# Attention scores and their sums one place earlier, and the residual of the first chunk added behind a copy

## The reference

```
x = x + attention(layernorm(x), ctx, ctx)    # 32 query heads, 8 key/value heads of width 128,
                                             # logits capped by 30*tanh(l/30), masked, softmax, then Wo
x = x + ffn(layernorm(x))                    # W_base, bias, and a top-2-of-8 mix of rank-16 LoRA experts
```

## Time and profile before

| | us |
|---|---|
| median of 3 runs (2152.28 to 2160.96) | 2158.23 |
| the profiled execution's own time | 2158.16 |
| its span, first to last instruction | 2156.4 |
| PE busy | 2132.3 |
| DVE busy | 1674.3 |
| ACT busy | 883.1 |
| POOL busy | 294.0 |

### The profile page before, as it was taken

One profiled execution on the slowest core, in us unless ns is written; L12 is line 12 of the kernel. 1 busy time (PEld: TensorE's weight loads), 2 busy tenths in 40 slices (PEclk: granted clock), 3 DMA queues, 4 the chain that ended last, 5 costly groups with the idle time before them and its releaser, 6 DMA issues.

```text
span 2156.4 us, 26390 instructions
## 1 busy us (share of the span) xinstructions
PE 2132.3 (99%) x9429; PEld 1729.3 (80%) x9429; DVE 1674.3 (78%) x2571; ACT 883.1 (41%) x1342; POOL 294.0 (14%) x359
## 2 busy tenths in 40 slices
PE   9999999999999999998999999999999999999999
PEld 7888888888888888876777877777787777888887
DVE  6976888888886666676877779997999879857443
ACT  3323243222241111155565556655666556423221
POOL 0350001111131000012101111111112111100000
PEclk9999999999999999999999999999999999999999
DMA  8698697665596665698666885689767965696741
GB/s 327 234 332 290 218 334 271 231 221 211 209 339 229 211 212 201 221 279 263 189 193 196 233 224 174 202 273 276 194 195 221 298 182 163 210 368 265 294 184 66
DMA packets 207987, 508.50 MB, mean 236 GB/s; under 512 B 20720, under 2 KB 54128, under 8 KB 205808
## 3 DMA queue, kind: packets, MB, share of 16 engines
q1 hardware_dynamic: 187376, 443.31, 62.7%
q0 software_dynamic: 20480, 63.50, 9.3%
HBM read 357.26 MB, written 149.16 MB: 235 GB/s over the span
## 4 chain that ended last, share of the span: by engine, by line
PE 87%; DMA 7%; DVE 3%; ACT 1%; issue 1%; SPq 0%; POOL 0%; DVEq 0%; ACTq 0%
PE ps L377 28%; PE ps L378 28%; PE ps L379 28%; DMA RB<-rD 3%; DMA rD<-r 2%; PE ps L920 1%; DMA X2D<-stg 1%; DMA raw<-gran 1%; DVE Y L990 1%; DMA Y<-xT 1%; DVE Rl L330 1%; DVE ps L330 0%; DVE ps L905 0%; DVE Pl L330 0%; DMA kraw<-ctxT 0%
## 5 line engine op out<-in xcount | busy, mean ns | idle before, releaser
L377 PE MATMUL ps<-Ah,Rh 128*128 128x512 f32 x1024 | 400.9, 391 | 4.2 <-DVE Y L990 4.2
L378 PE MATMUL ps<-Al,Rh 128*128 128x512 f32 x1024 | 399.9, 391 | 0.0
L379 PE MATMUL ps<-Ah,Rl 128*128 128x512 f32 x1024 | 399.5, 390 | 0.0
L379 PE MATMUL ps<-Xq,qW 128*128 128x512 f32 x896 | 348.6, 389 | 0.0
L377 PE MATMUL ps<-Xq,qW 128*128 128x512 f32 x896 | 348.5, 389 | 0.0
L378 PE MATMUL ps<-Xq,qW 128*128 128x512 f32 x896 | 348.5, 389 | 0.0
L330 DVE TENSOR_TENSOR Rl<-raw,Rh 128x1024 fp32r<-128x1024 f32 x174 | 212.2, 1220 | 57.6 <-ACT Rh L326 57.2
L326 ACT ACTIVATE Rh<-raw 128x1024 fp32r<-128x1024 f32 x176 | 185.5, 1055 | 154.6 <-PE ps L379 127.1
L377 PEld LDWEIGHTS ps<-Ah,Rh 128*128 128x128 f32 x1024 | 193.2, 189 | 46.8 <-DVE Y L990 4.6
L379 PEld LDWEIGHTS ps<-Ah,Rl 128*128 128x128 f32 x1024 | 193.1, 189 | 40.8
L378 PEld LDWEIGHTS ps<-Al,Rh 128*128 128x128 f32 x1024 | 193.2, 189 | 40.5
(11 more groups left out here) (217 smaller groups left out, 3881.7 us busy)
## 6 DMA issues: line engine op xcount, KB each, us to landing
raw<-gran SPq DMA_DIRECT2D x177, 512.0 KB, 5.6
QSD<-qW SPq DMA_DIRECT2D x64, 512.0 KB, 3.1
qD<-qt SPq DMA_DIRECT2D x128, 256.0 KB, 3.3
qW<-QSD SPq DMA_DIRECT2D x64, 512.0 KB, 3.7
qf<-qD SPq DMA_DIRECT2D x64, 512.0 KB, 8.5
RB<-rD POOLq DMA_DIRECT2D x128, 256.0 KB, 6.8
qraw<-gran SPq DMA_DIRECT2D x48, 512.0 KB, 4.3
kD<-kst SPq DMA_DIRECT2D x32, 512.0 KB, 3.8
```

What stands on the lines that cost most here:

```text
L377: put("pe", waits, lambda e: e.matmul(pe_out, lh, rh, start=first, stop=False, skip_group_check=more))
L378: put("pe", [], lambda e: e.matmul(pe_out, lh, rl, start=False, stop=False, skip_group_check=more))
L379: return put("pe", [], lambda e: e.matmul(pe_out, ll, rh, start=False, stop=last, skip_group_check=more), mark)
```

## The change

```diff
@@ o_evac @@
                 y = Y[:, n, :]
+                if (c, g) == (0, 0):
+                    a = put("act", [m] + y_free[n // 2], lambda e: e.activation(y, ps[b][:, :], ACT.Copy), cn("act_o"))
+                    bank_free[b] = [a]
+                    y_acc[c, n] = [tt("flex", y, y, Y2[:, n, :], ALU.add, [a, y_marks[c, n // 2]], "y")]
+                    y2_free.append(y_acc[c, n][0])
+                    return
                 a = put("dve", [m, y_marks[c, n // 2]] + y_acc.get((c, n), []),
                         lambda e: e.tensor_tensor(y, ps[b][:, :], y, ALU.add), cn("dve_y"))
@@ plan @@
         first = {0: ((-15, -14, -13, -12), -11, -9, (-7, -6, -5, -4)),
-                 1: ((-11, -9, -7, -6), -4, -2, (2, 3, 5, 6)),
+                 1: ((-11, -9, -7, -6), -4, -2, (1, 2, 4, 5)),
                  2: ((-4, -3, -1, 2), 4, 6, (8, 10, 12, 14))}
         for gi in range(len(groups)):
-            z = 8 * gi - 21
-            scores, sums, rows, values = first.get(gi, (range(z, z + 8, 2), z + 8, z + 11, range(z + 13, z + 21, 2)))
+            z = 8 * gi - 22
+            scores, sums, rows, values = first.get(gi, (range(z, z + 8, 2), z + 8, z + 12, range(z + 14, z + 22, 2)))
@@ at t == -2 @@
                     for j in range(4):
-                        y_load(0, j)
+                        y_marks[0, j] = dma(Y2[:, 2 * j:2 * j + 2, :], xT[0][:, 2 * j:2 * j + 2, :], y2_free, f"d_y{j}", 512)
```

## The result

| | before | changed |
|---|---|---|
| median, 15 runs each (us) | 2153.73 | 2169.97 |
| lowest to highest | 2146.58 to 2164.20 | 2161.86 to 2178.99 |
| the profiled execution, its span | 2158.16, 2156.4 | 2165.07, 2163.3 |

The changed kernel is slower: ratio 1.0069, 95% interval 1.0052 to 1.0085. The time lies above the range given, and the sign is the other one. The profiled execution of the changed kernel is at the fast end of its runs (2165 in 2162 to 2179), and that of the kernel before is above its median, so the two spans differ by 6.9 us where the medians differ by 16.2. The traces show the kinds of loss, but only part of the typical amount.

What follows compares the result with a forecast made beforehand. PE, busy 2132.3 of 2156.4 us, was taken as the bound, leaving only its waits and halved-clock stretches to win. 2158.2 - 4.5 (part one) - 0.9 (three waits) = 2152.8, predicted 2153 us; range 2144 to 2163.

Steps and rivals of the forecast that it cites:

- In all other groups PE never waited for an exponential, a bank or Al: Attention groups away from the three waits: bunching scores and sums takes some cover, cost 0, up to 3 us.
- the three changes of chunk: Near 1270, 1505 and 1737 us, where PE's sums waited for an exponential, 6.5 us together before the change.
- The chain moved with its start: Chain from a group's sums to RB: starting 2.7 us earlier, it was to end DVE's hold 2.7 us earlier.
- the second rival: RB lands no sooner while sums ask 2.7 us earlier; three waits grow 2.7 us each: 2163.5 us, chance 0.17.
- the draining picture: Small DMAs in RB's chain land only when loads in flight have drained, whenever issued; basis of the 2163 us rival.
- The waits at the changes of chunk: Three waits for exponentials were to be about 2.5, 0.5 and 2.8 us, 0.9 us won, slow clock left.
- The shorter hold of DVE: First change of chunk: DVE's hold for RB was to be some 5.4 us in place of 8.12.
- Part one: First chunk's x through Y2: removes place 3's 4.2 us wait and 1.7 us clock loss; 4.5 us won net.
- the 1.4 us wait at place 4: Group 2's sums were to wait 1.4 us for a late exponential, with the clock staying full.
- the three known waits: The sums' waits for exponentials near 1270, 1505 and 1737 us: 0.3 us won at each, 0.9 us together.
- the term put at 0: Cover lost by bunching work at even places in other groups: cost 0, up to 3 us.

Runs made afterwards that it cites:

- the first trace: Profile of the changed kernel itself, against the kernel before: profiled execution 2165.07 us, span 2163.3; median of its runs 2169.97 us.
- The run with stores counted late: Changed kernel with its planner counting each store X2D<-stg as landing 5 us later: 2146.30 us, ratio to the kernel before 0.9963.
- Sums back at -13: Changed kernel with sums of groups from 3 on returned to place 8 gi - 13, scores left moved: 2141.13 us, ratio to the kernel before 0.9946.
- the second trace: Profile from running the changed kernel again without any edit: 2172.04 us, ratio to the kernel before 1.0075.
- the run of part one alone: Kernel before with only the first chunk's x loaded through Y2, old table of places kept: 2156.05 us, ratio to the kernel before 1.0005.

## Why the prediction was wrong

- **The step that failed** is the sentence "In all other groups PE never waited for an exponential, a bank or Al", with "Cost 0; if the second layernorm's long operations take that cover, 1 us here and there, up to 3 us". No wait before doesn't mean room for one. From the end of a group's last exponential to the start of the fourth matmul of its sums there were 4.5 us in groups 4 to 9, but 1.2 to 2.0 us in groups 14, 16, 18, 22, 24, 26 and 30, and ACT's splits were held for 19.0 us by stores. The table gave the engines other lists, and in them the last scores of groups 17, 24 and 25 stand behind such holds: 9.8 us of waits in the first trace, with two slow stretches (3.4 us) and three broken sets. The run with stores counted late takes these three away, among others, and the loss is gone. The room left before would not have named the groups: 24 had 1.3 us, but 17 and 25, which waited longest, had 3.6 and 3.2. What could be seen was that holds of up to 3.6 us stood on ACT and that nothing said where they would fall in a new list.
- **The mechanism as a whole** was in my hands and not followed through. I wrote that sums and scores move together, so that an exponential is asked for 2.7 us earlier, and applied it at the three changes of chunk only. It holds in all 29 groups: the change put all the distance it won between sums and products (17.0 to 19.7 us), where PE had not waited, and none between scores and sums (6.1 us), where all three waits for exponentials were. Sums back at -13 gives the same place to the other side and wins 0.54% over before.
- **The chain moved with its start**, as forecast and against the second rival. From group 10's sums to its first multiplication by RB it took 29.8 us before (1239.92 to 1269.71) and 29.6 after (1231.88 to 1261.44), and the multiplication came 10.3 us behind its product before and 8.3 us after (last matmuls at 1259.46 and 1253.19): 2.0 us nearer, of the 2.7 forecast. The Trainium skill ("DMA: Bandwidth & Descriptors", "Queues, rings and completion order") has each DMA engine take turns between its queues packet by packet; these numbers fit that. They don't rule the draining picture out: the last keys loaded in the stretch landed some 9 us earlier as well.
- **The waits at the changes of chunk** stayed of their kind: 3.2 us for the first, none for the second, 0.7 us for the third in the first trace, against 2.7, 0.8 and 3.0; in the second trace none, 2.1 and 3.3. The forecast 2.5, 0.5 and 2.8 is within that spread, so it can't be told from no change, and the order behind the hold was right. The shorter hold of DVE that it rested on (5.4 us) did not come (7.80).
- **Part one**: copy ahead of the split, no wait for Y, full clock, all as forecast in the changed kernel. That the 1.4 us wait at place 4 was absent was luck, since the raw data came early; a wait of 0.4 us came at place 10. Taken alone part one is worth nothing (1.0005), and its trace has two waits for exponentials in place of the one for Y. What it is worth where none is late is not settled: 0.9946 against 0.9968, with overlapping intervals and other waits between the two.
- **The sum and the range.** For part one and the three known waits the first trace has no more than the 2153 allowed: 3.8 us of waits where 5.6 were left in the sum. What failed is the term put at 0, with at most 3 us. The range's upper end, 2163, came from a rival in which RB is late. No term had the broken sets, 1.0 us each.

## What to carry to other kernels

Before work is moved between two waits of a chain, measure the cover on each side (how long before the need the operand was ready, by group), and list the holds on every engine of the chain, with or without a wait of PE behind them. Where the lists are planned anew, a hold can fall elsewhere, so price each of them against the thinnest cover. A place more helps only on the side where the wait is; here it belonged between scores and sums, and the same table with one number changed went from 0.7% slower to 0.5% faster. In a kernel whose engines run lists planned ahead, a DMA counted faster than it lands parks a held instruction in front of urgent ones; counting it nearer the truth was worth nearly as much as the better table (0.9963 and 0.9946), and the two did not add up.

## What the runs showed of the hardware that was not expected

- Clock after a wait. I read 2.2 us as harmless and 2.7 us as not. It is no threshold: the same wait for Al near 978 us, some 2.6 us between the starts of two matmuls in either kernel, left the clock alone in the kernel before and was followed by the halved level in the run of part one alone (0.66 in the ten us from 975, 1.00 before). The kernel before shows the same by itself: after a wait of 2.4 us at 967 us, which I did not look at, the ten us from 966 had 0.83. And in the run of part one alone 1.87 us at 1013 left the clock alone and 1.89 us at 1041 did not (1.00 and 0.83 in the ten us behind). So the length of a wait doesn't tell whether the clock falls. Nor is the loss always the same: after the wait near 1264 us the ten us had 0.67 instead of 0.83, twice the loss.

```profile
966.92 0.72 PE L377 MATMUL ps<-Rh,Vh 128*128 128x512 f32 x1 [2.41 <-DVE Rl L330]
```

- A small DMA in a full stretch. The 8 KB links r<-rT and rD<-r took 8.0 and 7.7 us, at 987 and 990 us, where the engines' share was 0.62 and less, 2.2 and 1.7 us.
